# Attention block on one core: the feed-forward product with tokens on partitions, its result turned back by VectorE and stored in 128-byte runs

## The chip, the cores and the metric

The kernel runs on one core of one Trainium2 chip. The metric is the device time of one execution in microseconds (us). Every time below is one of those executions or comes from one execution taken by the hardware profiler.

## What is computed

The input is x, 16 images of 256 channels by 32x32 pixels in fp32. The reference, cut to what matters here (`B, C, H, W = 16, 256, 32, 32`; a token is one pixel):

```python
x = x + proj(softmax(q^T k / 16) v)          # q, k, v from a group norm of x; conv attention over 1024 tokens
t = x.reshape(B, C, H*W).transpose(0, 2, 1)  # tokens, 1024 x 256 for each image
n = layer_norm(t)
xn = n / |n|
t = t + softmax((xn xn^T)**2) n              # cosine attention
# feed-forward
n = layer_norm(t)
w = sign(weight - mean(weight)) * mean(|weight|)
y = n @ w + bias
y = round(clip(y, -1, 1) * 7) / 7
out = (t + y).transpose(0, 2, 1).reshape(B, C, H, W)
```

Products are made of two-part fp32 operands (a rounded high part and the rest, low), so that a matrix product is three TensorE products, or two where one operand is exact, as the signs of the weight are.

## The kernel before, in words

All five engines run hand-written instruction streams, one image ("batch" b) after the other, and meet at semaphores. A batch has two parts on each engine: `front(b, f, more)` and `back(b)`. `front` of batch b also carries the feed-forward work of the batch before, f = b - 1. The order of each engine's stream is written out by hand: a function's place in `front` is its place in the queue, and an engine that waits holds everything behind it.

TensorE's `front` (line 532): transposes of x, `queries`, `turn_ln2(f, 0)` (transposes of the layer-normed tokens), `values`, `ffn(f, 0)`, `turn_ln2(f, 1)`, `values`, `ffn(f, 1)`, then `turn_t(f, 0)`, `scores1(b, 0)`, `turn_t(f, 1)`, `scores1(b, 1)`, `turn_e1(b, 0)`. Then a loop over steps s = 1 to 8: `scores1(b, s + 1)`, `turn_e1(b, s)`, `product1(b, s - 1)`, and from s = 3 `turn_cos(b, s - 3)`. After it come the second attention's scores and, in `back`, its products.

The feed-forward work of a batch is done in two halves hf of 512 tokens. `ffn` (line 515) computes y with output channels on partitions and tokens along the free axis: for each of the two blocks m of 128 output channels, four matmuls with 512 moving columns. ScalarE's `ffn_out` (line 716) takes y from PSUM, multiplies by the scale and adds the bias, which lies per partition, and writes y_sb. VectorE's `clip` (953), GpSimd's `quantise` (1159) follow in y_sb. The residual sum tok has tokens on partitions, so `turn_t` (line 525) brings it to channels on partitions by eight fp32 transposes of 128x128 for each half, into the PSUM tile `turn`. VectorE's `output` (966) adds it to y_sb. SyncE's `store` (284) writes one half of 512 KB by one DMA, in runs of 2 KB.

Two more places matter. VectorE's step s = 1 runs `row_max(b, 2)`, `e1T_lo(b, 1)`, `gn_sums(b + 1, 1)`; step s = 2 begins with `residual1(b, 0)` (898), which reads the PSUM tile that product1(b, 0) filled and frees it: `product1(b, n)` (437) waits for the `t1_made` of n - 1. `turn_e1(b, 0)` (429) waits for `exp1(b, 0)` of ScalarE (665), which waits for `row_max(b, 0)` of VectorE (889), which waits for scores1(b, 0). After the last batch the feed-forward work has nothing beside it; its PSUM places and its order there are those of `LAST` and of the ends of the engines' streams.

## Time and profile before

| what | value |
|---|---|
| median of 3 executions | 1879.78 us (1879.66 to 1880.64) |
| profiled execution, first to last instruction | 1880.5 us |
| TensorE (PE) busy | 98% |
| VectorE (DVE), ScalarE (ACT), GpSimd (POOL) busy | 67%, 48%, 51% |
| DMA moved | 35.43 MB, mean 19 GB/s |
| one batch, from one x load to the next | 115.5 us |

The highest of the three executions, 1880.64 us, and the profiled span, 1880.5 us, agree to 0.1 us, so what lies around the span is at most about that; the median is 0.7 us below the span. The span runs from the first instruction on any engine to the last. In the rows further down, PE is TensorE's matmul side, PEld its weight loads, SPq SyncE's DMA queue, and "L528" a line of the kernel. A row of a timeline merges neighbouring instructions of one line; its first number is the start, its second the time that they take together. Matmuls overlap in their pipeline, so the pace of a group is read in the chain of waits and not from the mean of one.

### The profile page before, as it was taken

How to read it: one execution, taken by the hardware profiler on the slowest of the kernel's cores; microseconds unless marked ns; L12 is line 12 of the kernel's file. 1: busy time of each engine (PE TensorE's matmuls, PEld its weight loads, DVE VectorE, ACT ScalarE, POOL GpSimd, SP SyncE). 2: the span in 40 equal slices, each digit the busy share in tenths (PEclk: the TensorE clock that was granted, in tenths of full speed). 3: DMA queues.
4: the chain of work that ended last, by engine and by line, in shares of the span. 5: the costliest groups of instructions: out<-in, count | busy, mean ns of one | idle time of the engine just before them, and what ended most of it. 6: DMA issues, size and time to landing. Idle time of an engine off the chain costs nothing.

```text
span 1880.5 us, 36857 instructions
## 1 busy us (share of the span) xinstructions
PE 1840.7 (98%) x12834; PEld 1700.7 (90%) x12834; DVE 1268.5 (67%) x2516; ACT 906.0 (48%) x1444; POOL 958.9 (51%) x2262
## 2 busy tenths in 40 slices
PE   8999999999999999999999999999999999999997
PEld 7998999989899998999989999999998999989997
DVE  5676766667666676666767667676676766667566
ACT  3544536345463544635446354454544536355452
POOL 0654727447273472734637256372654727447272
PEclk9999999999999999999999999999999999999999
DMA  2000010000100001000010100001000010000000
GB/s 76 1 24 23 1 45 0 22 22 0 45 0 22 22 0 45 0 33 11 0 45 0 45 0 7 38 0 45 0 22 22 0 45 0 22 22 0 23 1 23
DMA packets 16416, 35.43 MB, mean 19 GB/s; under 512 B 2688, under 2 KB 4096, under 8 KB 16384
## 3 DMA queue, kind: packets, MB, share of 16 engines
q1 hardware_dynamic: 16384, 35.01, 5.1%
q8 instruction: 20, 0.33, 0.1%
q14 instruction: 12, 0.10, 0.0%
HBM read 18.23 MB, written 16.78 MB: 19 GB/s over the span
## 4 chain that ended last, share of the span: by engine, by line
PE 92%; DVE 5%; issue 2%; DMA 0%; ACT 0%; SPq 0%; POOL 0%; ACTq 0%; DVEq 0%; POOLq 0%
PE wide L322 33%; PE narrow L424 7%; PE narrow L426 7%; PE narrow L425 7%; PE turn L434 6%; PE wide L424 5%; PE wide L426 5%; PE wide L425 5%; PE narrow L322 5%; PE wide L520 3%; PE turn L481 2%; DVE prob L930 2%; PE turn L377 1%; PE narrow L452 1%; PE turn L511 1%
## 5 line engine op out<-in xcount | busy, mean ns | idle before, releaser
L322 PE MATMUL wide<-xn_hi,prob 128*128 128x512 f32 x1024 | 310.0, 404 | 0.0
L676 ACT ACTIVATE prob<-turn 128x1024 fp32r<-128x1024 f32 x128 | 131.3, 1026 | 322.1 <-PE turn L434 322.1
L1107 POOL TENSOR_TENSOR ln_v<-ln_mv,ln_eps 128x1 f32<-128x1 f32 x256 | 49.3, 193 | 455.8 <-DVE ln_mv L909 253.7
L690 ACT ACTIVATE ln<-tok,ln_shift,ln_r 128x256 f32<-128x256 f32 x128 | 77.0, 602 | 344.2 <-POOL ln_shift L1112 344.2
L891 DVE TENSOR_REDUCE neg_max<-wide 128x1 f32<-128x1024 f32 x128 | 156.4, 1222 | 122.9 <-PE wide L322 122.9
L424 PE MATMUL narrow<-prob 128*128 128x256 f32 x768 | 225.0, 293 | 0.0
L426 PE MATMUL narrow<-prob 128*128 128x256 f32 x768 | 217.0, 283 | 0.0
L425 PE MATMUL narrow<-prob 128*128 128x256 f32 x768 | 216.9, 282 | 0.0
L322 PEld LDWEIGHTS wide<-xn_hi,prob 128*128 128x128 f32 x1024 | 182.8, 188 | 35.4
L896 DVE TENSOR_TENSOR prob<-turn,prob 128x1024 fp32r<-128x1024 f32 x128 | 156.7, 1224 | 61.8 <-ACT prob L676 61.8
L669 ACT ACTIVATE expo<-wide,neg_max 128x1024 f32<-128x1024 f32 x128 | 142.6, 1114 | 58.2 <-DVE neg_max L891 58.0
L322 PE MATMUL wide<-xn_lo,prob 128*128 128x512 f32 x512 | 160.8, 395 | 0.0
L1147 POOL TENSOR_TENSOR prob<-expo,prob 128x128 fp32r<-128x128 f32 (+6 forms) x112 | 150.2, 1358 | 9.0 <-DVE prob L919 9.0
L424 PE MATMUL narrow<-val,prob 128*128 128x258 f32 x512 | 150.0, 293 | 0.0
L425 PEld LDWEIGHTS narrow<-prob 128*128 128x128 f32 x768 | 147.0, 191 | 0.0
L424 PEld LDWEIGHTS narrow<-prob 128*128 128x128 f32 x768 | 146.9, 191 | 0.0
L426 PEld LDWEIGHTS narrow<-prob 128*128 128x128 f32 x768 | 146.7, 191 | 0.0
L424 PE MATMUL wide<-val,prob 128*128 128x258 f32 x512 | 145.6, 284 | 0.0
L1136 POOL TENSOR_TENSOR cos_x<-ln_x,len_i 128x256 f32<-128x256 f32 x128 | 78.7, 615 | 130.7 <-ACT ln_x L683 126.6
L426 PE MATMUL wide<-val,prob 128*128 128x258 f32 x512 | 145.0, 283 | 0.0
L426 PE MATMUL narrow<-val,prob 128*128 128x258 f32 x512 | 145.0, 283 | 0.0
L425 PE MATMUL narrow<-val,prob 128*128 128x256 f32 x512 | 144.6, 282 | 0.0
(171 smaller groups left out, 5480.5 us busy)
## 6 DMA issues: line engine op xcount, KB each, us to landing
x_raw<-in_x SPq DMA_DIRECT2D x32, 512.0 KB, 4.0
out<-y_sb SPq DMA_DIRECT2D x32, 512.0 KB, 2.8
tok<-in_L_conv_qkv_w SPq DMA_DIRECT2D x1, 768.0 KB, 6.3
ln<-in_L_conv_proj_w SPq DMA_DIRECT2D x1, 256.0 KB, 6.8
ln<-in_L_ffn_weight SPq DMA_DIRECT2D x1, 256.0 KB, 4.3
out_bias<-in_L_conv_proj_b SPq DMA_DIRECT2D x1, 128.0 KB, 4.1
qkv_b_c<-in_L_conv_qkv_b SPq DMA_DIRECT2D x1, 3.0 KB, 6.6
norm_w_c<-in_L_conv_norm_w SPq DMA_DIRECT2D x1, 1.0 KB, 6.2
```

What stands on the lines that cost most here:

```text
L322: mm = pe.matmul(o, lhsT, r, start=first and i == 0, stop=last and i == len(parts) - 1)
L424: pe.matmul(o[:, 0:w], hi, value_hi(j), start=j == 0, stop=False)
L425: pe.matmul(o[:, 0:C], hi, value_lo(j), start=False, stop=False, skip_group_check=True)
L426: mm = pe.matmul(o[:, 0:w], lo, value_hi(j), start=False, stop=j == NT - 1)
L434: mm = pe.transpose(turn[:, tile(j)], expo[:, n % DEEP, tile(j)], ident[:, :])
L669: act.activation(expo[:, n % DEEP], wide[n % 2][:, :], ACT.Exp, bias=neg_max[:, n:n + 1], accum_out=row_sum1[:, n:n + 1]).then_inc(e1_made, 1)
L676: act.activation(eT_hi[:, n % 2], turn[:, :], ACT.Copy).then_inc(eT_hi_made, 1)
L690: act.activation(ln2[:, n], tok[:, n], ACT.Identity, bias=ln2_shift[:, n:n + 1], scale=ln2_r[:, n:n + 1]).then_inc(ln2_made, 1)
L891: dve.tensor_reduce(neg_max[:, n:n + 1], wide[n % 2][:, :], AX.X, ALU.max, negate=True).then_inc(max_made, 1)
L896: dve.tensor_sub(eT_lo[:, n % 2], turn[:, :], eT_hi[:, n % 2].bitcast(F32)).then_inc(eT_made, 1)
L1136: pool.tensor_tensor(cos_x[:, r], ln_x[:, r], len_i[:, n:n + 1].broadcast_to([P, C]), ALU.mult).then_inc(cos_made, 1)
L1147: pool.tensor_sub(prob[:, 1, J, row], expo[:, J % DEEP, row], prob[:, 0, J, row].bitcast(F32)).then_inc(p_made, 1)
```

## The change

`ffn` swaps its operands: the layer-normed tokens are the weights of the matmul and the signs the moving side. So y comes out with tokens on partitions and channels along the free axis, in 16 matmuls of 256 columns for each half instead of 8 of 512. `turn_t` and the semaphore of it are gone from TensorE, and so are its waits for `out_made`. `ffn_out` moves from ScalarE to VectorE as one `scalar_tensor_tensor` for each half, with a bias tile broadcast over the partitions (128 KB are loaded for it at the start instead of 1 KB). `output` adds tok and y_sb, both in SBUF, and then transposes the sum by VectorE in 32x32 blocks into `out_quad`, a view of ln2. After this, partition 32 tq + cc holds, for a block cb of 32 channels and a row of 32 pixels (one w-row of the image, of the four that a tile of 128 tokens has), 32 pixels in a run. `output(f, 0)` stands at the end of VectorE's step s = 1 and `output(f, 1)` at the end of s = 4. `store` waits for both halves, and issues 32 DMAs of 32 partitions, 256 runs of 128 bytes in each. `layer_norm2` of the next batch, which writes ln2 again, waits for all of them.

```diff
-    out_d = out.rearrange("b (k p) h w -> b p k (h w)", p=P)
+    outq_d = out.rearrange("b (cb cc) (n tq) w -> b tq cc cb n w", cc=Q, tq=P // Q)
...
+        out_quad = ln2[:, :, :].rearrange("p t c -> p (t c)").rearrange("p (cb n tt) -> p cb n tt", cb=C // Q, n=NT)
...
-            def store(f, hf):
-                sp.wait_ge(out_made, 2 * f + hf + 1)
-                sp.dma_start(out_d[f, :, :, hf * HALF:(hf + 1) * HALF], y_sb[:, hf]).then_inc(stored[hf], 16)
+            def store(f):
+                sp.wait_ge(out_made, 2 * f + 2)
+                for tq in range(P // Q):
+                    for cb in range(C // Q):
+                        sp.dma_start(outq_d[f, tq, :, cb], out_quad[tq * Q:(tq + 1) * Q, cb]).then_inc(stored, 16)
...
             def ffn(f, hf, places=PLACES):
                 pe.wait_ge(ln2T_made, 2 * f + hf + 1)
-                for m in range(KC):
+                for t in range(HT):
+                    o = places["y"][hf][t // 2][:, t % 2 * C:(t % 2 + 1) * C]
                     for k in range(KC):
                         for part in (tokT_lo, tokT_hi):
-                            mm = pe.matmul(places["y"][hf][m], sign_w[:, k, tile(m)],
-                                           part[:, k, hf * HALF:(hf + 1) * HALF],
+                            mm = pe.matmul(o, part[:, k, tile(HT * hf + t)], sign_w[:, k, :],
                                            start=k == 0 and part is tokT_lo, stop=k == KC - 1 and part is tokT_hi)
                 mm.then_inc(y_up, 1)
...
                 if f is not None:
                     pe.wait_ge(a_made, 2 * b + 2)
                     ffn(f, 1)
-                    turn_t(f, 0)
-                    pe.wait_ge(y_made, 4 * f + 2)
+                    pe.wait_ge(y_made, 2 * f + 1)
                 scores1(b, 0)
                 if f is not None:
-                    pe.wait_ge(out_made, 2 * f + 1)
-                    turn_t(f, 1)
-                    pe.wait_ge(y_made, 4 * f + 4)
+                    pe.wait_ge(y_made, 2 * f + 2)
                 scores1(b, 1)
...
-            def layer_norm2(b, n):
+            def layer_norm2(b, n, again=True):
                 act.wait_ge(ln2_scale, NT * b + n + 1)
+                if again and n == 0:
+                    act.wait_ge(stored, 16 * QUADS * b)
...
+            def ffn_out(f, hf, places=PLACES):
+                dve.wait_ge(y_up, 2 * f + hf + 1)
+                wholes = [wide[hf][:, :]] if places is PLACES else places["y"][hf]
+                step = HT // len(wholes)
+                for i, whole in enumerate(wholes):
+                    last = dve.scalar_tensor_tensor(
+                        y_sb[:, hf, i * step:(i + 1) * step], whole.rearrange("p (t c) -> p t c", t=step),
+                        w_mean[:, 1:2], ffn_bias[:, :].unsqueeze(1).broadcast_to([P, step, C]), ALU.mult, ALU.add)
+                last.then_inc(y_made, 1)
...
-            def output(f, hf, places=PLACES):
-                dve.wait_ge(tT_up, 2 * f + hf + 1)
-                dve.wait_ge(q_made, 2 * f + hf + 1)
-                dve.tensor_tensor(y_sb[:, hf], places["tT"][hf][:, :].rearrange("p (k t) -> p k t", k=KC), y_sb[:, hf],
-                                  ALU.add).then_inc(out_made, 1)
+            def output(f, hf):
+
+                i, some = 2 * f + hf, slice(HT * hf, HT * (hf + 1))
+                dve.wait_ge(q_made, i + 1)
+                dve.tensor_tensor(y_sb[:, hf], tok[:, some], y_sb[:, hf], ALU.add).then_inc(sum_made, 1)
+                dve.wait_ge(ln2T_up, 2 * f + 2)
+                dve.wait_ge(sum_made, i + 1)
+                dve.transpose(out_quad[:, :, some].rearrange("p cb n tt -> p n cb tt"),
+                              y_sb[:, hf].rearrange("p n (cb cc) -> p n cb cc", cc=Q)).then_inc(out_made, 1)
...
@@ -1012,6 +1003,8 @@
                         e1T_lo(b, s)
                     if more and s == 1:
                         gn_sums(b + 1, 1)
+                    if f is not None and s in (1, 4):
+                        output(f, s // 4)
...
@@ -1051,13 +1044,15 @@
             ln2T_lo(f, 0, LAST)
             for n in range(NT - 2, NT):
                 residual2(f, n)
+            ffn_out(f, 0, LAST)
             clip(f, 0)
             ln2T_lo(f, 1, LAST)
             quantise(f, 0)
-            output(f, 0, LAST)
+            ffn_out(f, 1, LAST)
             clip(f, 1)
+            output(f, 0)
             quantise(f, 1)
-            output(f, 1, LAST)
+            output(f, 1)
```

What this does to the order on two engines, at three places. The lines of the changed kernel are shifted against those of the kernel before (L325 is the old L322, L869 the old L891, L874 the old L896, L882 the old L904). The names: `wide`, `turn` and `narrow` are PSUM tiles, `prob` holds the two parts of the query and value operands and of the exponentials, `expo` the exponentials.

TensorE from the last matmul of `ffn(f, 1)` into `scores1(b, 1)`, before:

```order
L520 MATMUL wide<-tokT_hi,sign_w 128x512
L528 MATMUL turn<-ident,tok 128x128 x8
L566 ISA
L322 MATMUL wide<-xn_hi,prob 128x512 x2
L322 MATMUL wide<-xn_lo,prob 128x512 x2
L322 MATMUL wide<-xn_hi,prob 128x512 x4
L322 MATMUL wide<-xn_lo,prob 128x512 x2
L322 MATMUL wide<-xn_hi,prob 128x512 x2
L528 MATMUL turn<-ident,tok 128x128 x8
L571 REGISTER_ALU
L322 MATMUL wide<-xn_hi,prob 128x512 x2
```

and now:

```order
L524 MATMUL wide<-sign_w,tokT_hi 128x256
L325 MATMUL wide<-xn_hi,prob 128x512 x2
L325 MATMUL wide<-xn_lo,prob 128x512 x2
L325 MATMUL wide<-xn_hi,prob 128x512 x4
L325 MATMUL wide<-xn_lo,prob 128x512 x2
L325 MATMUL wide<-xn_hi,prob 128x512 x4
L325 MATMUL wide<-xn_lo,prob 128x512 x2
```

Both groups of eight transposes of tok (L528) are gone. scores1(b, 1) follows scores1(b, 0) directly; its first rows are merged with the last of scores1(b, 0) into the second x4.

VectorE from behind `ln2T_lo(f, 1)` (L950; the new list begins with it, as L928) to `row_max(b, 0)`, before:

```order
L955 TENSOR_SCALAR y_sb<-y_sb 128x1024
L885 REGISTER_ALU
L886 TENSOR_TENSOR prob<-narrow,prob 128x2x256
L885 REGISTER_ALU
L886 TENSOR_TENSOR prob<-narrow,prob 128x2x256
L954 REGISTER_ALU
L955 TENSOR_SCALAR y_sb<-y_sb 128x1024
L969 TENSOR_TENSOR y_sb<-turn,y_sb 128x1024
L890 ISA
L891 TENSOR_REDUCE neg_max<-wide 128x1
L969 TENSOR_TENSOR y_sb<-turn,y_sb 128x1024
```

and now:

```order
L928 TENSOR_TENSOR tokT_lo<-turn,tokT_hi 128x2x512
L936 SCALAR_TENSOR_TENSOR y_sb<-wide,w_mean,ffn_bias 128x1024
L943 TENSOR_SCALAR y_sb<-y_sb 128x1024
L863 REGISTER_ALU
L864 TENSOR_TENSOR prob<-narrow,prob 128x2x256
L863 REGISTER_ALU
L864 TENSOR_TENSOR prob<-narrow,prob 128x2x256
L936 SCALAR_TENSOR_TENSOR y_sb<-wide,w_mean,ffn_bias 128x1024
L943 TENSOR_SCALAR y_sb<-y_sb 128x1024
L868 ISA
L869 TENSOR_REDUCE neg_max<-wide 128x1
```

Two `scalar_tensor_tensor` from `wide` have come in, each with a clip behind it, and the two sums from `turn` have left this stretch.

VectorE in step s = 1 and at the start of s = 2, before:

```order
L890 REGISTER_ALU
L891 TENSOR_REDUCE neg_max<-wide 128x1
L896 TENSOR_TENSOR prob<-turn,prob 128x1024
L854 BN_STATS gn_stats<-x_raw 128x6 x2
L803 REGISTER_ALU
L804 MEMSET carrier 128x1
L856 BN_AGGR gn_mv<-gn_stats 128x2
L902 RECIPROCAL inv_sum<-row_sum 128x1
L904 SCALAR_TENSOR_TENSOR tok<-narrow,inv_sum,x_tok 128x256
```

and now:

```order
L869 TENSOR_REDUCE neg_max<-wide 128x1
L874 TENSOR_TENSOR prob<-turn,prob 128x1024
L832 BN_STATS gn_stats<-x_raw 128x6 x2
L781 REGISTER_ALU
L782 MEMSET carrier 128x1
L834 BN_AGGR gn_mv<-gn_stats 128x2
L958 TENSOR_TENSOR y_sb<-tok,y_sb 128x1024
L961 STREAM_TRANSPOSE ln<-y_sb 128x4x8x32
L880 RECIPROCAL inv_sum<-row_sum 128x1
L882 SCALAR_TENSOR_TENSOR tok<-narrow,inv_sum,x_tok 128x256
```

The sum of tok and y_sb and the transpose (L958, L961) stand between the statistics of the next batch's x and `residual1(b, 0)`. The same pair stands behind e1T_lo(b, 4) in step s = 4, with no statistics ahead of it.

## Rows read from the trace of the kernel before

**Rows 1.** The page, part 1: busy time, share of the span and instructions of TensorE.

```profile
PE 1840.7 (98%) x12834; PEld 1700.7 (90%) x12834; DVE 1268.5 (67%) x2516; ACT 906.0 (48%) x1444; POOL 958.9 (51%) x2262
```

**Rows 2.** The chain of waits: start us, us, what; hand-over from one batch to the next.

```profile
1182.21 2.80 PE narrow L322 x24
1185.01 1.87 PE wide L520 x8
1186.88 0.87 PE turn L528 x8
1187.75 2.79 PE wide L322 x12
1190.55 0.87 PE turn L528 x8
```

**Rows 3.** Timeline of VectorE, same batch: start us, us, what [idle before it <-releaser].

```profile
1183.30 1.23 DVE L950 TENSOR_TENSOR tokT_lo<-turn,tokT_hi 128x1024 fp32r<-128x1024 f32 x1 [1.83 <-ACT tokT_hi L712]
1184.64 0.69 DVE L955 TENSOR_SCALAR y_sb<-y_sb 128x1024 f32<-128x1024 f32 x1
1185.25 1.28 DVE L886 TENSOR_TENSOR prob<-narrow,prob 128x512 fp32r<-128x512 f32 x2
...
1190.59 1.23 DVE L891 TENSOR_REDUCE neg_max<-wide 128x1 f32<-128x1024 f32 x1 [0.36 <-PE wide L322]
```

**Rows 4.** Timeline of GpSimd, same batch.

```profile
1187.09 1.05 POOL L1165 TENSOR_SCALAR y_sb<-y_sb 128x1024 f32<-128x1024 f32 x1
```

**Rows 5.** Timeline of batch 0, which has no feed-forward work before its scores.

```profile
36.20 1.23 DVE L891 TENSOR_REDUCE neg_max<-wide 128x1 f32<-128x1024 f32 x1 [1.47 <-PE wide L322]
...
38.48 0.19 ACT L669 ACTIVATION_READ_ACCUMULATOR expo<-wide,neg_max 128x1 f32 x1
...
38.81 1.06 PE L434 MATMUL turn<-ident,expo 128*128 128x128 f32 x8
```

**Rows 6.** VectorE's groups by line and shape: xcount | busy us, mean ns.

```profile
L924 DVE TENSOR_TENSOR prob<-expo,prob 128x512 fp32r<-128x512 f32 x32 | 82.0, 2563 | 1.1
...
L881 DVE SCALAR_TENSOR_TENSOR prob<-wide,a_bias,prob 128x1024 fp32r<-128x1024 f32 x32 | 40.8, 1276 | 1.5 <-ACT prob L656 1.5
...
L808 DVE TENSOR_TENSOR xn_lo<-x_norm,xn_hi 128x1024 fp32r<-128x1024 f32 x2 | 2.4, 1220 | 1.7 <-ACT xn_hi L652 1.7
```

**Rows 7.** Timeline of VectorE, batch before: sums of residual1(b, 0) and residual1(b, 3).

```profile
1087.09 0.48 DVE L904 SCALAR_TENSOR_TENSOR tok<-narrow,inv_sum,x_tok 128x256 f32<-128x256 f32 x1
...
1106.63 0.48 DVE L904 SCALAR_TENSOR_TENSOR tok<-narrow,inv_sum,x_tok 128x256 f32<-128x256 f32 x1
```

**Rows 8.** Timeline of TensorE: first matmul of product1(b, 1) and of product1(b, 4).

```profile
1089.56 0.36 PE L424 MATMUL narrow<-prob 128*128 128x256 f32 x1
...
1110.04 0.36 PE L424 MATMUL narrow<-prob 128*128 128x256 f32 x1
```

**Rows 9.** Timeline of the end of the program, all engines.

```profile
1867.49 1.23 DVE L950 TENSOR_TENSOR tokT_lo<-wide,tokT_hi 128x1024 fp32r<-128x1024 f32 x1 [0.22 <-ACT tokT_hi L712]
...
1871.40 6.26 SPq L285 DMA_DIRECT2D out<-y_sb  x2
...
1872.30 1.45 ACT L721 ACTIVATE y_sb<-narrow,ffn_b_c,w_mean 128x512 f32<-128x512 f32 x2 [4.84 <-PE narrow L520]
...
1876.04 1.22 DVE L969 TENSOR_TENSOR y_sb<-wide,y_sb 128x1024 f32<-128x1024 f32 x1
```

**Rows 10.** Timeline of SyncE's queue: the next x load.

```profile
1173.14 0.92 SPq L281 DMA_DIRECT2D x_raw<-in_x  x2
```

**Rows 11.** Timeline of ScalarE: first layer_norm2 of this batch.

```profile
1155.13 0.60 ACT L690 ACTIVATE ln<-tok,ln_shift,ln_r 128x256 f32<-128x256 f32 x1 [9.75 <-POOL ln_shift L1112]
```

**Rows 12.** DMA queue, 8 to 8.5 us, mostly 4-byte packets: packets, MB, share of 16 engines.

```profile
q1 hardware_dynamic: 1013, 0.06, 142.4%
```

**Rows 13.** DMA queue, 6 to 7 us, packets of 1 KB.

```profile
q1 hardware_dynamic: 371, 0.38, 108.2%
```

**Rows 14.** DMA queue, 1878 to 1879 us, packets of 2 KB of the last store.

```profile
q1 hardware_dynamic: 153, 0.31, 81.7%
```

More of the change, by code:

```diff
@@ L36 @@
 BANK = 512
+Q = 32
 GROUPS = 8
@@ L56, in build @@
     NP = len(PARTS)
-    assert KC == 2 and N == 2 * BANK and C // GROUPS == 32
+    assert KC == 2 and N == 2 * BANK and C // GROUPS == 32 and W == Q
     scale = float(C) ** -0.5
     x_d = x.rearrange("b (k p) h w -> b p k (h w)", p=P)
-    out_d = out.rearrange("b (k p) h w -> b p k (h w)", p=P)
+    outq_d = out.rearrange("b (cb cc) (n tq) w -> b tq cc cb n w", cc=Q, tq=P // Q)
     with ExitStack() as ctx:
@@ L248, in build @@
         q_made = sem("q_made")
-        tT_up = sem("tT_up")
+        sum_made = sem("sum_made")
         out_made = sem("out_made")
-        stored = [sem("stored0"), sem("stored1")]
+        stored = sem("stored")
+        QUADS = (P // Q) * (C // Q)
         QKV_LOADS, NORM_LOADS, FFN_LOADS = 16 * 3, 16 * 2, 16 * 3
@@ L306, in _ @@
                 reload(b + 1)
-                store(b - 1, 0)
-                store(b - 1, 1)
+                store(b - 1)
             for f in (B - 2, B - 1):
-                store(f, 0)
-                store(f, 1)
-            sp.wait_ge(stored[0], 16 * B)
-            sp.wait_ge(stored[1], 16 * B)
+                store(f)
+            sp.wait_ge(stored, 16 * QUADS * B)
         @block.tensor
@@ L516, in ffn @@
                 pe.wait_ge(ln2T_made, 2 * f + hf + 1)
-                for m in range(KC):
+                for t in range(HT):
+                    o = places["y"][hf][t // 2][:, t % 2 * C:(t % 2 + 1) * C]
                     for k in range(KC):
                         for part in (tokT_lo, tokT_hi):
-                            mm = pe.matmul(places["y"][hf][m], sign_w[:, k, tile(m)],
-                                           part[:, k, hf * HALF:(hf + 1) * HALF],
+                            mm = pe.matmul(o, part[:, k, tile(HT * hf + t)], sign_w[:, k, :],
                                            start=k == 0 and part is tokT_lo, stop=k == KC - 1 and part is tokT_hi)
                 mm.then_inc(y_up, 1)
-            def turn_t(f, hf, places=PLACES):
-                for k in range(KC):
-                    for t in range(HT):
-                        mm = pe.transpose(places["tT"][hf][:, k * HALF + t * P:k * HALF + (t + 1) * P],
-                                          tok[:, HT * hf + t, tile(k)], ident[:, :])
-                mm.then_inc(tT_up, 1)
             def front(b, f, more):
@@ L632, in _ @@
             ffn(f, 0, LAST)
-            turn_t(f, 0, LAST)
             turn_ln2(f, 1, LAST)
             ffn(f, 1, LAST)
-            turn_t(f, 1, LAST)
         @block.scalar
@@ L714, in ln2T_hi, with front @@
                                ).then_inc(ln2T_hi_made, 1)
-            def ffn_out(f, hf, reuse, places=PLACES):
-                act.wait_ge(y_up, 2 * f + hf + 1)
-                if reuse:
-                    act.wait_ge(stored[hf], 16 * f)
-                for m in range(KC):
-                    act.activation(y_sb[:, hf, m], places["y"][hf][m], ACT.Identity,
-                                   bias=ffn_b_c[:, m:m + 1], scale=w_mean[:, 1:2]).then_inc(y_made, 1)
-            def front(b, f, more, reuse=True):
+            def front(b, f, more):
                 query_hi(b, 0)
@@ L732, in front @@
                     ln2T_hi(f, 1)
-                    ffn_out(f, 0, reuse)
                 value_hi(b, 2)
                 value_hi(b, 3)
-                if f is not None:
-                    ffn_out(f, 1, reuse)
                 exp1(b, 0)
@@ L762, in front, with back @@
                         layer_norm1(b, NT - 1)
-            def back(b, more):
+            def back(b, more, again=True):
                 if more:
@@ L768, in back @@
                 for n in range(NT):
-                    layer_norm2(b, n)
+                    layer_norm2(b, n, again)
             act.wait_ge(prep_pe, 1)
@@ L780, in _ @@
             front(0, None, True)
-            back(0, True)
-            front(1, 0, True, reuse=False)
+            back(0, True, again=False)
+            front(1, 0, True)
             with act.Fori(2, B - 1) as b:
@@ L793, in _ @@
                 layer_norm2(f, n)
-            ffn_out(f, 0, True, LAST)
             ln2T_hi(f, 1, LAST)
-            ffn_out(f, 1, True, LAST)
         @block.vector
@@ L986, in front @@
                     ln2T_lo(f, 1)
+                    ffn_out(f, 0)
                     clip(f, 0)
@@ L990, in front @@
                 if f is not None:
+                    ffn_out(f, 1)
                     clip(f, 1)
-                    output(f, 0)
                 row_max(b, 0)
-                if f is not None:
-                    output(f, 1)
                 row_max(b, 1)
```

17 lines of the change are left out of this document (8 added, 9 removed).

## The prediction

> **What bounds the kernel now.** The page first: TensorE is busy 98% of the span, VectorE 67%, GpSimd 51%, ScalarE 48% [rows 1]. The reader is to see one engine without gaps, so that work taken from it counts in full unless a new wait takes its place. The chain of waits in order of time says the same of the stretch that is edited: each TensorE group begins where the last ends, with nothing of another engine between [rows 2]. It also gives the pace, which the mean of a pipelined matmul doesn't: 24 matmuls of 256 columns in 2.80 us (0.117 each), 8 of 512 in 1.87 (0.234 each), 8 fp32 transposes in 0.87. The timelines of VectorE, GpSimd and ScalarE then show how far ahead of TensorE they are at each place that is touched [rows 3, 4, 7, 8], batch 0 shows the same scores without transposes between them [rows 5], and the end of the program and the DMA rows show what nothing covers [rows 9, 12 to 14].
>
> The sum is made against the profiled execution, 1880.5 us in span, 0.7 above the median of 1879.8.
>
> **TensorE: the transposes go.** 2 groups of 0.87 us [rows 2] in each of the 15 batches whose feed-forward work lies in a later `front`: 30 x 0.87 = 26.1 us less. The last batch's two groups lie at the end, beside ScalarE's and VectorE's longer work, and count nothing.
>
> **TensorE: the product.** 16 x 0.117 = 1.87 us in place of 8 x 0.234 = 1.87 [rows 2]. The columns are the same in number, and the 24 matmuls of the values have this very shape. Cost 0.
>
> **VectorE takes ffn_out.** The nearest row is a `scalar_tensor_tensor` of 128x1024 from PSUM at 1.28 us [rows 6]. I lay the new order over the old times. `ln2T_lo(f, 1)` ends at 1184.53 [rows 3]. ffn_out(f, 0) then ends at 1185.8, clip (0.69) at 1186.5, the two value_lo (1.28 together) at 1187.7 [rows 3]. scores1(b, 0) now may begin at 1186.88 [rows 2], and its wait for ffn_out(f, 0) is over 1.1 us before. ffn_out(f, 1) ends at 1188.9. scores1(b, 1) needs it at about 1189.7, so this is covered too. clip(f, 1) would end at 1189.6, and row_max(b, 0), 0.87 us earlier than in the trace, is due at 1190.59 - 0.87 = 1189.72 [rows 3]. That fits by a tenth.
>
> What stands behind row_max has no room left. In batch 0 the transposes of turn_e1 begin 2.61 us after row_max, 0.14 after the exponential's last instruction ends [rows 5], while scores1(b, 1) lasts 2.79 [rows 2]; before the change the 0.87 us of turn_t(f, 1) was the room. So each delay of row_max(b, 0) reaches TensorE. One is in sight. GpSimd's second quantise pass ends 2.81 us after the end of the first clip (1184.64 + 0.69, and 1187.09 + 1.05) [rows 3, 4], now at 1189.3, and clip(f, 1) falls on it. The trace has VectorE operations stretched beside GpSimd's: a sum of 128x512 with two SBUF inputs takes 2563 ns on average, one of 128x1024 at the start of the program 1220 [rows 6]. If the clip is held until 1189.3, it ends at 1189.96 and row_max is 0.2 us late: 15 x 0.2 = 3.0 us, and if it isn't held, 0. I take 3.0. The Trainium skill (SBUF — State Buffer, "Who interferes with whom") says that a VectorE operation in a two-port mode and a GpSimd instruction exclude each other and the second to start waits for the whole of the first; by that rule this term is 3.0, without it 0.
>
> **VectorE in step s = 1.** The pair of sum and transpose is put ahead of residual1(b, 0). The sum with two SBUF inputs is the row of 1220 ns [rows 6]; GpSimd has no work then, its layer norm waits for this very residual. The trace has no transpose on VectorE. Its bounds are 0.69 us, the clip of as many elements and the fastest pass there is [rows 3], and 2.45 us, twice a pass at the usual pace. I take 1.22, as nearly all passes over 1024 fp32 elements have it. The pair then moves what follows by 1.23 + 0.04 + 1.22 less 0.08 of overlap = 2.4 us. residual1(b, 0)'s sum ended at 1087.57 [rows 7] and now ends at 1090.0. product1(b, 1) waits for it and began at 1089.56 [rows 8]. The 2.0 us of room there are gone, and TensorE stands 0.5 us, in the 14 batches that also have gn_sums in this step: 14 x 0.5 = 7.0 us. Bounds: 0 and 14 x 1.7 = 24 us.
>
> **VectorE in step s = 4.** The same 2.4 us ahead of residual1(b, 3), which ended at 1107.11 [rows 7]; product1(b, 4) begins at 1110.04 [rows 8], 2.9 us later, and VectorE had idled 0.6 before. Cost 0. It is covered even if GpSimd holds the sum for one of its short operations.
>
> **ScalarE** loses four activations in a batch. It isn't waited for there: 0. Its new wait, that layer_norm2 needs all stores, holds the whole queue. The stores begin when output(f, 1) is done, at about 1108.4; layer_norm2 is at 1155.13 [rows 11]. 46 us are room for 14 to 44 us of stores (below). Cost 0. The next x load, queued behind the stores on SyncE, is at 1173.14 [rows 10]: 0. The larger bias load at the start, 128 packets of 1 KB at 371 in a us [rows 13], is under 0.4 us, and VectorE idles longer before it needs anything more: 0.
>
> **The end, on VectorE.** The second half's y is there at 1872.30 [rows 9], as now, since turn_ln2 and ln2T_lo (1867.49) don't change. Then come two ffn_out pieces (1.3 together), the clip (0.73 with its wait), the first half's sum and transpose (2.5), two quantise passes (1.46), and the second half's sum and transpose (2.5): 1880.8. Before, the last sum ended at 1876.04 + 1.22 = 1877.26 [rows 9]. Cost 3.5 us.
>
> **The end, stores.** Before, the second half's store waited for the last sum (1877.26), its issue ended at 1871.40 + 6.26 = 1877.66 [rows 9], and the span ended at 1880.5, 3.2 us after the sum. Now 32 DMAs go out after both halves. Two x loads take 0.92 us to issue [rows 10], 0.46 each, at 256 packets each as here. The last goes out 31 x 0.46 = 14.3 us after the first, and then has 1 us less to move. Cost 13.3 us, if the packets keep up: each DMA gives each of the 16 DMA engines 16 packets in 0.46 us, 29 ns for each. Bounds of a 128-byte packet: 11 ns, of small ones (16 x 0.5 x 1.424 / 1013) [rows 12], and 85 ns, of 2 KB (16 x 0.817 / 153) [rows 14]; packets of 1 KB have 47 [rows 13]. By size it lies nearest to the small ones, so the queue bounds: 14.3 us, up to 512 x 85 = 43.5.
>
> Sum: -26.1 + 3.0 + 7.0 + 3.5 + 13.3 = +0.7 us; profiled 1881.2, median **1880.5**. The transposes' 26.1 us are spent: 10 in the batches, 16.8 once at the end.
>
> **The rivals.**
> 1. *128-byte stores are bound by the packets, slower.* Only one store stands bare, the last. Decides from 29 ns a packet. At 47 ns, 512 x 0.047 = 24.1 us in place of 14.3: 1890.3; at 85 ns 1910. For it: none of the packets that the trace shows at 11 ns is a write to HBM. Against: price falls with size in the three rows. The Trainium skill (DMA: Bandwidth & Descriptors, Specifications) speaks against this change here: below 512 bytes a DMA does a read-modify-write and loses line rate; it gives no price, and by it this case is the one that comes. Chance 0.25.
> 2. *The transpose takes two passes, slower.* 2.45 us: product1(b, 1) waits 1.7, 17.2 us more, and 2.5 at the end: 1900. Nothing in the trace speaks for or against. Chance 0.10.
> 3. *The room in front of turn_e1 is missed in full, slower.* If VectorE comes to row_max(b, 0) 0.87 us late, the transposes' second 0.87 is returned each time: 13 in place of 3.0, 1890.5. It needs VectorE slower than its rows by 0.8 us over five operations. Chance 0.08.
> 4. *The transpose is fast, faster.* At 0.69 us the stop at product1(b, 1) is gone and the end is 1.1 shorter: 1872.4. Decides from 0.72 us a transpose. For it: the clip has such a pace in the same buffer. Against: VectorE's sums and its reduction of 1024 fp32 elements all take 1.22 to 1.28 [rows 3, 6, 9]. Chance 0.12.
>
> The forecast itself has 0.45, with 1875 to 1886 as its own range.
>
> **Numbers.** A measurement of this kernel tells about 0.2%, 3.8 us. Faster by more: rival 4 and 0.04 of the forecast, 0.16. Within: 0.37. Slower: 0.47 (rivals 1 to 3 and 0.04). The range is 1872 (rival 4) to 1900 (rival 2, and rival 1 up to 66 ns); left out are the ends of these, some 0.15.
>
> **What would show it.** No transposes of tok, and scores1(b, 1) directly behind scores1(b, 0); a batch of 115.5 - 1.74 + 0.2 + 0.5 = 114.5 us; TensorE waiting 14 times 0.5 us at product1's first matmul for VectorE's tok, and under 0.3 at turn_e1; VectorE's transposes at 1.2 us; 0.46 from DMA to DMA on SyncE; and some 17 us from the last transpose to the end. Wrong would be: a wait of ScalarE for a store, a batch as long as before, an end of 10 or of 30 us.

## The result and the profile after

The changed kernel takes 1887.5 us (median of 5 runs, 1886.34 to 1889.02), the kernel before beside it 1880.14 (5 runs, 1879.66 to 1881.03). The ratio is 1.0039 (95% interval 1.0027 to 1.0052): slower by 7.4 us. The forecast was 1880.5 us, which is 0.7 above the 1879.8 that it was made from.

| | before | after |
|---|---|---|
| profiled execution, its own time | 1880.64 us | 1887.64 us |
| its span | 1880.5 us | 1885.9 us |
| TensorE busy | 98% | 96% |
| batch to batch, from SyncE's x loads | 115.52 us | 114.47 us |
| last transpose (before: last sum) to the end of the span | 3.2 us | 22.6 us |

The page of after, part 1, answers to [rows 1]. TensorE (PE) has lost 24 us of busy time and VectorE (DVE) has gained 71:

```profile
PE 1816.5 (96%) x12834; PEld 1688.3 (90%) x12834; DVE 1339.9 (71%) x2582; ACT 865.3 (46%) x1380; POOL 964.6 (51%) x2262
```

**The interior is faster, as forecast.** SyncE's x load is a mark that comes once in a batch. Before, the timeline of its queue has (start us, us, what):

```profile
248.99 0.92 SPq L281 DMA_DIRECT2D x_raw<-in_x  x2
...
1635.27 0.92 SPq L281 DMA_DIRECT2D x_raw<-in_x  x2
```

and after, with the stores between them:

```profile
246.76 0.87 SPq L284 DMA_DIRECT2D x_raw<-in_x  x2
...
1048.03 0.86 SPq L284 DMA_DIRECT2D x_raw<-in_x  x2
1097.81 24.36 SPq L290 DMA_DIRECT2D out<-ln  x32
1162.49 0.86 SPq L284 DMA_DIRECT2D x_raw<-in_x  x2
...
1620.36 0.86 SPq L284 DMA_DIRECT2D x_raw<-in_x  x2
```

From the first to the last row are 12 batches: 1386.28 / 12 = 115.52 us before, 1373.60 / 12 = 114.47 after. The forecast was 114.5. The stores of a batch take SyncE 24.4 us and are out 40 us before the next x load, so they cost nothing here.

The chain of waits of after, at the hand-over between the same two batches, answers to [rows 2]:

```profile
1168.83 1.91 PE wide L524 x16
1170.73 0.87 PE turn L514 x8
1171.61 2.83 PE narrow L325 x24
1174.44 1.92 PE wide L524 x16
1176.36 5.61 PE wide L325 x24
1181.97 0.89 PE turn L437 x8
```

Both groups of transposes of tok are gone, and the two groups of scores run as one, 5.61 us. The product in its new shape (L524) takes 1.91 to 1.92 us where 8 matmuls took 1.87 (the first product of the batch 1.89), and the values' 24 matmuls 2.83 where they took 2.80. The first wait that was forecast, in front of turn_e1, hardly is one: 5.61 is 0.03 more than twice the 2.79 of [rows 2], and the chain of before has 2.81 for the second of the two groups, which leaves 0.01.

**The second wait is there.** The table of waits of TensorE (us in total, times, longest us):

```profile
PE narrow L427 <- DVE tok L882: 3.7, 14, 0.3
```

and VectorE's timeline in step s = 1, answering to the first row of [rows 7], shows what stands ahead of residual1's sum (L882):

```profile
1190.20 1.17 DVE L958 TENSOR_TENSOR y_sb<-tok,y_sb 128x1024 f32<-128x1024 f32 x1
1191.48 1.25 DVE L961 STREAM_TRANSPOSE ln<-y_sb 128x1024 f32<-128x1024 f32 x1
1192.65 0.12 DVE L880 RECIPROCAL inv_sum<-row_sum 128x1 f32<-128x1 f32 x1
1192.80 0.48 DVE L882 SCALAR_TENSOR_TENSOR tok<-narrow,inv_sum,x_tok 128x256 f32<-128x256 f32 x1
```

The transpose takes 1.25 us, forecast 1.22.

**The end is where the time goes.** Timeline of after, VectorE's last work and SyncE's queue, answering to [rows 9]:

```profile
1849.86 1.22 DVE L928 TENSOR_TENSOR tokT_lo<-wide,tokT_hi 128x1024 fp32r<-128x1024 f32 x1 [1.37 <-ACT tokT_hi L703]
...
1862.06 1.25 DVE L961 STREAM_TRANSPOSE ln<-y_sb 128x1024 f32<-128x1024 f32 x1
1863.33 20.78 SPq L290 DMA_DIRECT2D out<-ln  x32
```

From the start of ln2T_lo to the end of the last transpose are 13.45 us, 3.7 more than the 9.77 to the last sum before (forecast 3.5). Then 32 DMAs take 20.78 us to issue, 0.65 each, and 1.8 us after the end of the last issue (1863.33 + 20.78 = 1884.11) the span ends. What the DMA engines did between 1864 and 1884 us (packets, MB, share of 16 engines):

```profile
q1 hardware_dynamic: 8160, 0.98, 31.9%
```

They are busy a third of the time: 0.319 x 16 x 20 us / 8160 = 12.5 ns for a packet, far from the 29 ns at which rival 1 would have decided.

The mean granted clock of TensorE fell from 0.998 to 0.992, but that is not where the time went. In both runs it is 1.00 (2.4 GHz) up to 1840 us. At the end TensorE has to wait for ScalarE and VectorE (in after from 1848.8 to 1851.1 us), and the clock falls to 0.50 (1.2 GHz) under most of the last product. It does so in both, and the product takes nearly as long before as after (from the two chains of waits):

```profile
1868.77 3.51 PE narrow L520 x8
1851.14 3.60 PE narrow L524 x16
```

In the last 31 us of after the clock is 0.54 on average, but TensorE has nothing more to do there.

### The profile page after: what moved, and what is told of

The parts are those of the page before. It is cut to its first block, busy times and chain, and to the rows that moved or that the text cites. A ratio compares the mean times of both kernels' runs of the same rounds, so it can differ in the third digit from the quotient of the medians.

```text
span 1885.9 us, 38092 instructions
## 1 busy us (share of the span) xinstructions
PE 1816.5 (96%) x12834; PEld 1688.3 (90%) x12834; DVE 1339.9 (71%) x2582; ACT 865.3 (46%) x1380; POOL 964.6 (51%) x2262
## 4 chain that ended last, share of the span: by engine, by line
PE 83%; DVE 10%; issue 4%; ACT 1%; DMA 0%; SPq 0%; DVEq 0%; POOL 0%; POOLq 0%
PE wide L325 28%; PE narrow L427 7%; PE narrow L429 7%; PE narrow L428 7%; PE wide L427 5%; PE wide L429 5%; PE wide L428 5%; PE turn L437 5%; PE narrow L325 5%; PE wide L524 3%; PE turn L484 2%; DVE gn_stats L832 2%; DVE prob L908 2%; PE turn L380 1%; PE narrow L455 1%
## 5 line engine op out<-in xcount | busy, mean ns | idle before, releaser
L325 PE MATMUL wide<-xn_hi,prob 128*128 128x512 f32 x1024 | 305.3, 402 | 0.0
L427 PE MATMUL narrow<-prob 128*128 128x256 f32 x768 | 225.3, 293 | 3.7 <-DVE tok L882 3.7
L869 DVE TENSOR_REDUCE neg_max<-wide 128x1 f32<-128x1024 f32 x128 | 156.1, 1220 | 91.4 <-PE wide L325 91.0
L325 PEld LDWEIGHTS wide<-xn_hi,prob 128*128 128x128 f32 x1024 | 184.4, 188 | 36.5
L874 DVE TENSOR_TENSOR prob<-turn,prob 128x1024 fp32r<-128x1024 f32 x128 | 156.5, 1223 | 51.4 <-ACT prob L665 51.4
L325 PE MATMUL wide<-xn_lo,prob 128*128 128x512 f32 x512 | 160.9, 395 | 0.0
L427 PEld LDWEIGHTS narrow<-prob 128*128 128x128 f32 x768 | 146.7, 191 | 7.0 <-DVE tok L882 7.0
L427 PE MATMUL narrow<-val,prob 128*128 128x258 f32 x512 | 149.8, 293 | 0.0
L427 PE MATMUL wide<-val,prob 128*128 128x258 f32 x512 | 145.6, 284 | 0.0
L428 PE MATMUL wide<-val,prob 128*128 128x256 f32 x512 | 144.5, 282 | 0.0
```

The lines of the kernel that those rows point to most:

```text
L325: mm = pe.matmul(o, lhsT, r, start=first and i == 0, stop=last and i == len(parts) - 1)
L427: pe.matmul(o[:, 0:w], hi, value_hi(j), start=j == 0, stop=False)
L428: pe.matmul(o[:, 0:C], hi, value_lo(j), start=False, stop=False, skip_group_check=True)
L869: dve.tensor_reduce(neg_max[:, n:n + 1], wide[n % 2][:, :], AX.X, ALU.max, negate=True).then_inc(max_made, 1)
L874: dve.tensor_sub(eT_lo[:, n % 2], turn[:, :], eT_hi[:, n % 2].bitcast(F32)).then_inc(eT_made, 1)
```

## The experiments

The four questions were: is the interior gain the whole price of the transposes; what are the two waits in front of turn_e1 and product1(b, 1) worth; is the end bound by SyncE's queue or by the packets; and what sets 0.65 us for a DMA.

### The transposes put back: a_turn_back

```diff
                     ffn(f, 1)
+                    turn_tok(0)
                     pe.wait_ge(y_made, 2 * f + 1)
                 scores1(b, 0)
                 if f is not None:
+                    turn_tok(1)
                     pe.wait_ge(y_made, 2 * f + 2)
```

turn_tok(hf) is the old 8 transposes of tok into `turn`, with no reader.

> The changed kernel with the two groups of 8 fp32 transposes of tok put back on TensorE at their old places, into PSUM that nobody reads. Theory (the transposes were worth their whole 0.87 us a group inside the batches, and the changed kernel loses it elsewhere): 15 x 2 x 0.87 = 26 us more, less the 15 x 0.19 = 2.9 us of waiting at turn_e1 that their 0.87 us would cover again: about 23 us more than the changed kernel's 1887.5, so 1910 to 1911, and the waits at turn_e1 gone while the 14 x 0.5 us at product1's first matmul stay. Rival (interior gain smaller than its price, part of the transposes was hidden under VectorE anyway): 10 to 18 us more, with the waits at turn_e1 or scores1(b, 1) taking up what is missing.

Measured: 1913.03 us (4 runs, 1911.75 to 1913.88), 25.5 more than the changed kernel. The timeline of SyncE's queue:

```profile
247.91 0.87 SPq L284 DMA_DIRECT2D x_raw<-in_x  x2
...
1642.33 0.86 SPq L284 DMA_DIRECT2D x_raw<-in_x  x2
```

gives 116.20 us a batch, 1.735 more, and two groups of 0.87 are 1.74. The rival falls: each transpose counted in full. The theory was 2.5 us short, for it gave 2.9 us back at turn_e1, and there was nothing to give back. In this trace the wait at turn_e1 (0.19 us of idle time of the weight loads, 15 times, in the changed kernel) is gone, and still the batch is longer by the full two groups.

### The clip behind the maximum: c_clip_late

```diff
                     ffn_out(f, 1)
-                    clip(f, 1)
                 row_max(b, 0)
+                if f is not None:
+                    clip(f, 1)
```

> The changed kernel with clip(f, 1) moved from before row_max(b, 0) to behind it. Theory (row_max(b, 0) is late since the clip stands in front of it, 0.69 to 0.91 us, and turn_e1 waits 0.19 us for the exponential, 15 times): row_max(b, 0) starts 0.9 us earlier, the waits at turn_e1 go and the time falls by 3 us, to 1884.7. Rival (scores1(b, 0)'s own end or ScalarE's queue sets row_max and the exponential): the time stays within 1 us. A GpSimd quantise pass that begins 1.2 us later costs nothing in either, unless layer_norm1 waits behind it on GpSimd (it doesn't start before residual1(b, 0), 10 us later).

Measured: 1889.04 us (5 runs, 1886.78 to 1890.08), span of the profiled run 1885.7, period 114.50 against 114.47: no gain. VectorE's timeline says why (last bracket: idle before it, and its releaser):

```profile
1176.49 1.27 DVE L936 SCALAR_TENSOR_TENSOR y_sb<-wide,w_mean,ffn_bias 128x1024 f32<-128x1024 f32 x1
1178.72 1.23 DVE L869 TENSOR_REDUCE neg_max<-wide 128x1 f32<-128x1024 f32 x1 [0.96 <-PE wide L325]
1179.86 0.68 DVE L943 TENSOR_SCALAR y_sb<-y_sb 128x1024 f32<-128x1024 f32 x1
```

With the clip out of the way, row_max(b, 0) only waits 0.96 us for TensorE, and it begins 3.00 us after scores1(b, 0) begins (1175.72), as it did in the changed kernel: 3.01 (1176.19 to 1179.20). The clip ended there at the very moment at which the scores were ready, and so looked like the cause. The theory falls, the rival holds: row_max(b, 0) begins 3.01 us after scores1(b, 0), turn_e1 2.60 us after row_max(b, 0), and these 5.61 us are as long as the two groups of scores (2.79 and 2.81 in the chain of before) to 0.01 us, whatever VectorE does ahead of them.

### The transpose taken out of step s = 1: b_split_output

```diff
-                    if f is not None and s in (1, 4):
-                        output(f, s // 4)
+                    if f is not None and s == 1:
+                        output(f, 0, turn_too=False)
+                    if f is not None and s == 4:
+                        transposed(f, 0)
+                    if f is not None and s == 5:
+                        output(f, 1)
```

output's transpose has become a function of its own, transposed(f, hf). The sum must stay in s = 1, since residual1(b, 0) overwrites tok.

> The changed kernel with output(f, 0) split: its sum stays in step s = 1, its transpose goes to s = 4, and output(f, 1) goes from s = 4 to s = 5. Theory (product1(b, 1) waits 0.5 us for residual1(b, 0), which stands behind the sum and the transpose on VectorE): what stands ahead of residual1(b, 0) shrinks by 1.25 us, more than the 0.5 of waiting, so the 14 waits of 0.50 us at L427 go and the time falls by 7 us, to 1880.5. The stores start some 6 us later and still end before layer_norm2. Rival (the waits are replaced by others further on in the batch, at s = 4 or 5 or in front of turn_e1): the time falls by less than 3 us and a new wait for VectorE shows at product1 or turn_e1.

Measured: 1880.3 us (11 runs, 1879.01 to 1883.47), 7.2 less than the changed kernel and level with the one before (ratio 0.9999, 0.999 to 1.0008). The row L427 <- DVE tok has left the table of waits, nothing has come in its place, and a batch takes 113.95 us, 0.51 less:

```profile
244.99 0.87 SPq L284 DMA_DIRECT2D x_raw<-in_x  x2
...
1612.43 0.86 SPq L284 DMA_DIRECT2D x_raw<-in_x  x2
```

So 14 x 0.5 us is what this wait costs. The table of waits gives 3.7 us for the matmuls alone. The weight loads of the same line, in part 5 of the page of after, have 7.0 (the last two numbers):

```profile
L427 PEld LDWEIGHTS narrow<-prob 128*128 128x128 f32 x768 | 146.7, 191 | 7.0 <-DVE tok L882 7.0
```

But the weight loads' 2.9 us at turn_e1 were worth nothing, so the period is the better measure of a wait.

### The last stores on two queues: d_two_queues

```diff
-            for f in (B - 2, B - 1):
-                store(f)
+            store(B - 2)
+            sp.wait_ge(out_made, 2 * B)
+            for tq in (0, 1):
+                for cb in range(C // Q):
+                    sp.dma_start(outq_d[B - 1, tq, :, cb], out_quad[tq * Q:(tq + 1) * Q, cb]).then_inc(stored, 16)
...
+            act.wait_ge(out_made, 2 * B)
+            for tq in (2, 3):
+                for cb in range(C // Q):
+                    act.dma_start(outq_d[f, tq, :, cb], out_quad[tq * Q:(tq + 1) * Q, cb]).then_inc(stored, 16)
```

> The changed kernel with the last batch's 32 stores dealt to two queues, 16 on SyncE's and 16 on ScalarE's. Theory (a queue takes 0.65 us for each of these DMAs, and the queues work side by side): the tail shrinks by 16 x 0.65 = 10.4 us, to 1877. Rival 1 (what they need is shared, the packets or the DMA engines, though these are busy only 30%): no change, 1887.5, with each issue on either queue taking 1.3 us. Between: ScalarE's queue is slower for each DMA, a gain of 5 to 9 us.

Measured: 1878.68 us (10 runs, 1876.01 to 1880.4), 8.8 less, where 10.4 was expected. In the profiled run, the fastest of the ten, the end of the last transpose (1861.57) is 12.6 us before the end of the span, 10.0 less than the 22.6 of the changed kernel. The timelines of the two queues:

```profile
1861.59 10.42 SPq L318 DMA_DIRECT2D out<-ln  x16
```

```profile
1861.60 10.79 ACTq L781 DMA_DIRECT2D out<-ln  x16
```

and the DMA queues between 1862 and 1872 us:

```profile
q1 hardware_dynamic: 3808, 0.46, 30.1%
q10 hardware_dynamic: 3791, 0.46, 29.7%
```

Each queue keeps its 0.65 to 0.67 us a DMA, and the engines are now 60% busy. They had room for twice as many packets; the queue's issuing was the bound. The Trainium skill (DMA: Bandwidth & Descriptors, Rules for kernel authors) says that dealing DMAs to several engines brings no bandwidth and saves only the time to issue them. On the time to issue the trace agrees: here it was 10 us on the path. Between 1862 and 1872 us the engines also moved more, 92 GB/s where one queue had given them 49, but only because they had stood idle for the rest of the time.

### What sets 0.65 us: e_half_dmas, f_long_runs, g_128_parts

All three change the last batch's stores alone.

```diff
 e_half_dmas
+                    for n in (0, NT // 2):
+                        sp.dma_start(outq_d[B - 1, tq, :, cb, n:n + NT // 2],
+                                     out_quad[tq * Q:(tq + 1) * Q, cb, n:n + NT // 2]).then_inc(stored, 16)
 f_long_runs
+                    sp.dma_start(outf_d[B - 1, :, cb, tq * C:(tq + 1) * C],
+                                 out_quad[tq * Q:(tq + 1) * Q, cb].rearrange("p n tt -> p (n tt)")
+                                 ).then_inc(stored, 16)
 g_128_parts
+                    sp.dma_start(outg_d[B - 1, cb % 2, cb // 2, :, n:n + 2],
+                                 out_quad[:, cb, n:n + 2]).then_inc(stored, 16)
```

> The changed kernel with the last batch's stores cut in two: 64 DMAs of 128 runs of 128 bytes in place of 32 of 256. Theory P (SyncE's queue takes its 0.65 us for the packets, 2.5 ns for each of 256): 64 x 0.33, the same 20.8 us of issuing, the time unchanged at 1887.5. Theory D (a fixed price for each DMA): 64 x 0.65 = 41.7 us, 20.8 us more, 1908. Between the two the pitch p of a DMA gives both parts: fixed + 128 x slope = p, fixed + 256 x slope = 0.65.

> The changed kernel, with the last batch's 32 stores writing 32 runs of 1 KB each from the same 32 partitions in place of 256 runs of 128 bytes; the last batch's values land in other places than they should. Theory P (the price goes by packets): 32 in place of 256 packets, issue of each DMA under 0.15 us, the tail up to 16 us shorter, 1872 or more if the landing sets it. Theory D (fixed price for each DMA): 0.65 us each as before, 1887.5. Rival B (the price goes by bytes or by partitions, 32 KB and 32 of them here as before): also 0.65.

> The changed kernel, with the last batch's 32 stores reading two runs of 128 bytes from each of 128 partitions in place of eight from each of 32; number of DMAs, runs and bytes are unchanged, the values land in other places than they should. Theory P (256 packets set the price, wherever they lie): 0.65 us each, 1887.5. Rival S (the shape sets it: few partitions with many runs each are slow, as the loads and stores over 128 partitions with 256 packets took only 0.34 to 0.46 us): 0.35 to 0.46 each, the tail 6 to 9 us shorter, 1879 to 1881.5.

Measured, one run each: 1899.17, 1881.29 and 1883.19 us. The timelines of SyncE's queue, in this order:

```profile
1864.90 30.49 SPq L319 DMA_DIRECT2D out<-ln  x64
```

```profile
1863.10 14.75 SPq L319 DMA_DIRECT2D out<-ln  x32
```

```profile
1862.96 16.28 SPq L319 DMA_DIRECT2D out<-ln  x32
```

| the DMA | packets | partitions | us a DMA |
|---|---|---|---|
| changed kernel, 8 runs of 128 bytes per partition | 256 | 32 | 0.65 |
| e_half_dmas, 4 runs of 128 bytes | 128 | 32 | 0.48 |
| f_long_runs, 1 run of 1 KB | 32 | 32 | 0.46 |
| g_128_parts, 2 runs of 128 bytes | 256 | 128 | 0.51 |

No theory holds alone. A price for packets only would leave e_half_dmas unchanged and bring f_long_runs under 0.15; a fixed price would make e_half_dmas 20.8 us longer, and it issues for 9.7 longer. Between the first two rows the sum splits into about 0.30 us for a DMA and 1.4 ns for a packet, but then f_long_runs should take 0.34, and g_128_parts, with the same packets, 0.65. The shape counts as well. The x load, from which the prediction took its price, has its 256 packets in 128 partitions, 2 runs in each, and one such issue lasts 0.37 us. In g_128_parts, with the same partitions and runs but 128 bytes in each run, one lasts 0.47, and in the changed kernel, with 8 runs in each of 32 partitions, 0.61 (medians). So more than half of the gap, 0.14 of 0.24 us, goes with how the packets lie and not with their number. (In g_128_parts their places in the output differ too.) What is shown, by one run of each: a DMA of 16 to 32 KB costs its queue 0.46 us or more in every shape tried, and this kernel's shape is the dearest of them. The rule behind the rest stays open.

### The kernel before once more: before_again

No edit. In the changed kernel's trace the first row of the queue shown above comes 2.2 us earlier than in that of before (246.76 against 248.99). 1.0 of it is the gain of a batch, but 1.2 stand already at the x load before it (23.21 against 24.41), where little but the load of the bias was changed.

> The kernel before, profiled once more. The two profiled executions differ at the start of the program: SyncE's x load of batch 2 is issued at 24.41 us before the change and at 21.6 to 23.2 in all profiles since, though that part was not changed. Theory (the start varies from run to run): this profile has it at another time than 24.41, with its span shorter by as much, 1878 to 1880.5, and the batch period at 115.52. Rival (the change itself made the start faster, for example by the bias load): 24.4 again and a span of 1880.5.

Measured: 1883.29 us, span 1881.6, and the x load that the expectation speaks of (the row holds those of batches 1 and 2) at 25.39:

```profile
25.39 109.98 SPq L281 DMA_DIRECT2D x_raw<-in_x  x4
```

The period is 115.53. The direction that was expected was wrong, but the start does vary: in the profiles of this study that x load lies between 21.6 and 25.4 us, at 24.64 for e_half_dmas, whose start is that of the changed kernel. So the same start can take as long as that of before, and nothing shows that the change made it shorter; with two profiles of before, 24.41 and 25.39, and nine of ten others at 23.22 or less, nothing excludes it either. A single profile is good to some 2 us only. Also, each time beside these runs is 1.7 us or more above its span, this one too (1883.29 and 1881.6), where the first profile of before has 0.1. What was read from that one profile, that at most 0.1 us lies around the span, doesn't hold for any other execution whose span is known; why it differs stays open. The sum was made against a span that was long by about 1.6 us for its time. With it the spans of the two profiled executions differ by 5.4 us and their times by 7.0 (the medians by 7.4).

### The old end, and the best of both: k_old_tail, j_split_old_tail

k_old_tail does the last batch the old way, with a column ffn_b_c loaded for it. The core of it, on TensorE and SyncE:

```diff
-            ffn(f, 0, LAST)
+            ffn_old(f, 0, LAST)
+            turn_t(f, 0, LAST)
             turn_ln2(f, 1, LAST)
-            ffn(f, 1, LAST)
+            ffn_old(f, 1, LAST)
+            turn_t(f, 1, LAST)
...
+            for hf in range(2):
+                sp.wait_ge(out_made, 2 * (B - 1) + hf + 1)
+                sp.dma_start(out_d[B - 1, :, :, hf * HALF:(hf + 1) * HALF], y_old[:, hf]).then_inc(stored, 16)
```

> The changed kernel, with the last batch alone done in the old way (channels on partitions, ScalarE's ffn_out, TensorE's transposes of tok, two stores of 512 KB). Theory (of the changed kernel's end, 13.45 us from ln2T_lo(f, 0) to the last transpose and 22.6 us from there to the end of the span, the old end takes 9.77 and 3.24): 23.0 us less, 1864.5, and 15.7 us faster than the kernel before. Rival (part of the end is common to both, e.g. stores of batch 14 still in the queue, or the interior gain is smaller than the periods say): 10 to 18 us less.

> The kernel of k_old_tail with the split of output(f, 0) of b_split_output as well, the version to beat both. Theory: the two edits touch different places and add up, 1864.5 - 7.2 = 1857.3, ratio to the kernel before 0.988, period of a batch 113.95. Rival (they meet somewhere): less than 5 us below k_old_tail.

Measured: k_old_tail 1862.42 us (4 runs, 1861.87 to 1863.04), ratio to the kernel before 0.9899 (0.9883 to 0.9916), 25.1 less than the changed kernel where 23.0 was expected. Its end, on VectorE and SyncE's queue (span 1860.1):

```profile
1847.52 1.23 DVE L962 TENSOR_TENSOR tokT_lo<-wide,tokT_hi 128x1024 fp32r<-128x1024 f32 x1 [0.22 <-ACT tokT_hi L729]
...
1855.65 1.22 DVE L1089 TENSOR_TENSOR y_sb<-wide,y_sb 128x1024 f32<-128x1024 f32 x1
```

```profile
1856.90 0.40 SPq L322 DMA_DIRECT2D out<-y_sb  x1
```

From ln2T_lo to the end of the span are 12.6 us, in the changed kernel 36.0 (1849.86 to 1885.9): 23.4 less. The rest is 1.2 us at the start, which varies, and a period shorter by 0.08 us (114.39). Its batches have the same instructions as the changed kernel's; in the chain of waits the values' groups take 2.81 there in place of 2.83 and the second product 1.89 in place of 1.92. Why the same matmuls run a little faster in this build stays open.

j_split_old_tail adds the split of output(f, 0): 1854.32 us (4 runs, 1854.22 to 1854.69), ratio 0.9855 (0.9839 to 0.9872), 1857.3 expected. It is 8.1 below k_old_tail, so the two edits add up, and the kernel beats both: 26 us faster than before, 33 faster than the changed one. Its batches take 113.87 us, 0.52 less than those of k_old_tail, which is 7.3 us for 14 of them:

```profile
246.09 0.87 SPq L288 DMA_DIRECT2D x_raw<-in_x  x2
...
1612.49 0.86 SPq L288 DMA_DIRECT2D x_raw<-in_x  x2
```

Of the rest, the two profiled runs show 0.95 us at the end, and it goes with TensorE's clock. The last product has the same 8 matmuls in both; here are the chains of waits, and the windows of the same stretches (the number behind POOL's is the granted clock), k_old_tail first:

```profile
1848.80 3.09 PE narrow L540 x8
1849.00:1851.00 2.00, 2.00 (x7) 1.59 (x7) 1.86 (x3) 0.00 (x0) 0.00 (x0) 0.66 0.00 0
1851.00:1853.00 2.00, 2.00 (x10) 1.71 (x9) 0.41 (x1) 1.08 (x2) 0.00 (x0) 0.50 0.31 121
```

```profile
1842.57 2.14 PE narrow L540 x8
1843.00:1845.00 2.00, 2.00 (x13) 1.64 (x12) 1.86 (x3) 0.26 (x1) 0.00 (x0) 1.00 0.03 8
```

At the lower clock the product takes 0.95 us longer. Whether the split or chance kept the clock up in this execution isn't shown.

## Why the prediction came out as it did

Each term of the sum against what the runs and traces show (for the second, 114.467 less 115.523 - 1.735 + 0.513 + 0.03 leaves 0.136 us a batch).

| term | forecast, us | measured, us | from |
|---|---|---|---|
| 30 groups of transposes | -26.1 | -26.0 | a_turn_back: 15 x 1.735; 25.5 in time |
| product and values | 0 | about +2.0 | what the period leaves, 15 x 0.136; the chains show 0.02 and 0.05 in the two products, 0.02 to 0.03 in each values group |
| room in front of turn_e1 | +3.0 | +0.4 at most | 15 x 0.03; c_clip_late: nothing to gain |
| sum and transpose at s = 1 | +7.0 | +7.2 | b_split_output |
| the end, VectorE | +3.5 | +3.7 | timelines |
| the end, stores | +13.3 | +19.4 | 22.6 - 3.2 |
| sum | +0.7 | +6.7 | time: +7.4; span: +5.4, with a start that is 1.2 shorter in the profile of after |

**The places were right.** The interior gains 1.06 us a batch (12.68 / 12; forecast 1.04), and the end eats it. That the interior came out so close is in part luck: the wait at turn_e1, forecast at 0.2 us a batch, is nearly nothing, and the product and the values, forecast at nothing, cost 0.14. Nor was the direction of the whole really forecast, since +0.7 is less than the 3.8 us that the prediction calls the measurement's own. The step that failed is the price of issuing a store: "Two x loads take 0.92 us to issue [rows 10], 0.46 each, at 256 packets each as here." The number of packets was the same and the price wasn't. Nor is 0.46 the pace of that row: one of the two issues lasts 0.37, so the second begins 0.92 - 0.37 = 0.55 us after the first, and half of the row is neither. The stores take 0.65 each, and 31 x 0.19 = 5.9 us is nearly all of what the forecast lacked. f_long_runs and g_128_parts show that 0.46 to 0.51 was to be had from other shapes of as many bytes: the row that was taken has its packets in 128 partitions, the stores in 32. The reasoning took one row for a price and gave its own term no range from above on the queue's side, only on the packets'.

**Rival 1, the packets: not so.** The packets took 12.5 ns, close to the 11 that [rows 12] gave for small ones, and d_two_queues put twice as many through the engines in the same time. Yet the time came out near where the mildest form of this rival had it (1890.3): the right neighbourhood for a wrong reason, which only the share of the DMA engines and the second queue tell apart. The Trainium skill (DMA: Bandwidth & Descriptors, Specifications) has a loss of line rate below 512 bytes; no wait in any run here can be put down to it, since the queue came first.

**The wait at turn_e1: wrong in size and cause.** The forecast put 0.2 us a batch on a clip held by GpSimd. The clip was stretched beside GpSimd's pass, 0.91 us in place of 0.69 (timelines of after):

```profile
1177.58 1.05 POOL L1160 TENSOR_SCALAR y_sb<-y_sb 128x1024 f32<-128x1024 f32 x1
1178.27 0.91 DVE L943 TENSOR_SCALAR y_sb<-y_sb 128x1024 f32<-128x1024 f32 x1
1179.20 1.22 DVE L869 TENSOR_REDUCE neg_max<-wide 128x1 f32<-128x1024 f32 x1
```

With the clip moved, all 32 of them take 0.69 (0.684 to 0.695). But it was hidden under scores1(b, 0). By the rule of the Trainium skill (SBUF — State Buffer, "Who interferes with whom") the clip would have waited for the end of the pass at 1178.63 and ended at 1179.32. It ended at 1179.18, 0.14 sooner, so the trace doesn't show quite that, and either way nothing followed for the time.

**The product at nought: small miss.** 16 matmuls of 256 columns take 1.91 and 1.92 us in a batch, where the two groups of 8 of 512 take 1.89 and 1.87. The rate of 0.117 from the values' group does not quite carry over: 0.119 to 0.120 here. Nor need the whole 0.136 us a batch be the new operand order: k_old_tail, with the same matmuls in its batches, has a period 0.08 us shorter.

**Rivals 2 and 4** are settled by the trace: the transpose takes one usual pass, 1.25 us. **Rival 3** has no part of its 10 us.

**The costs of nought** held: ScalarE's wait for the stores never bites (first layer_norm2 at 1259.05, the stores of that batch issued by 1212.28 + 24.36 = 1236.64), and nor does step s = 4.

## What to carry to other kernels

A DMA has a price on the queue that issues it, which neither its bytes nor its packets give alone. Many small ones are free while work covers them and stand bare after the last instruction, so treat the last iteration as a kernel of its own: with the old layout there, the same change is worth 1.0% instead of costing 0.4%, and with the transpose moved to s = 4 as well 1.5%. Price an issue from a row of the same shape (partitions and runs in each, not only the number of packets), or give it a range on both sides. And put a long operation that has no hurry (the transpose) where nobody waits behind it, even if its partner (the sum) has to stay.

## What the runs showed beyond that

- Within the batches the same stores take 24.36 / 32 = 0.76 us each, at the end 0.65 (20.78 / 32), though a single instruction lasts 0.58 there and 0.61 at the end. In front of each of the 448 stores of the loop over the batches the trace has two register instructions of SyncE, 37 and 29 ns, which the 64 stores behind the loop don't have. Whether they are all of the 0.11 us wasn't tested.
- At the start of the program the same groups of matmuls run at different speed in different executions: 8 of 128x256 took 3.44 us in before and 1.97 in after, but 3.65 in e_half_dmas, whose start is that of after. The granted clock is 1.00, the 2.4 GHz level, for all these stretches, so this number doesn't tell them apart. The cause wasn't sought. Here is one of either, from the timelines of TensorE:

```profile
15.36 3.44 PE L347 MATMUL wide<-expo,tok 128*128 128x256 f32 x8
```

```profile
14.01 1.97 PE L353 MATMUL wide<-expo,tok 128*128 128x256 f32 x8
```

  (before, and d_two_queues, whose start is that of the changed kernel.)
- A wait in the table can be a wait in name: the trace gives turn_e1's weight loads 0.19 us of waiting for the exponential, 15 times in the changed kernel, and taking away what was ahead of it on VectorE gained nothing, while product1's row gave 3.7 us for the matmuls, 7.0 for the weight loads, and was worth 7.2.
